# Two-bit threshold search, one packing pass and experts spread over the attention steps

## The reference

```python
xn = _layernorm(x)                                  # x: 1 x 2048 x 128
q, k, v = split(xn @ W_attn.T + b_attn)             # 16 heads of 8
att = softmax(where(causal, q @ k.T / sqrt(8), -inf))
y = (att @ v) @ W_proj.T + b_proj
probs = softmax(xn @ choice_w.T)                    # 2048 x 8
G, I = top_k(probs.T, 512)                          # per expert
h = silu(xn[I] @ w1)                                # 512 x 256, per expert
ffn = zeros.at[I].add(G[..., None] * (h @ w2))
out = x + y + ffn
```

## Time and profile before

| | us |
|---|---|
| median of 3 runs (361.47 to 363.31) | 362.79 |
| the profiled execution | 363.24 |
| its span | 361.5 |
| granted clock of TensorE, mean | 0.947 |

### The profile page before, as it was taken

One profiled execution on the slowest core, in us unless ns is written; L12 is line 12 of the kernel. 1 busy time (PEld: TensorE's weight loads), 2 busy tenths in 40 slices (PEclk: granted clock), 3 DMA queues, 4 the chain that ended last, 5 costly groups with the idle time before them and its releaser, 6 DMA issues.

```text
span 361.5 us, 6404 instructions
## 1 busy us (share of the span) xinstructions
PE 309.8 (86%) x2453; PEld 106.4 (29%) x2453; DVE 214.9 (59%) x558; ACT 289.5 (80%) x328; POOL 127.4 (35%) x122
## 2 busy tenths in 40 slices
PE   1684839699899769897998999999999999999970
PEld 0442802122222212221223232423242333232470
DVE  6939995966765878759777443251345433426443
ACT  1197747589999859897999999899999999998700
POOL 8520241920000000008760007584868251606060
PEclk9999558789999989999999999999999999999995
DMA  6035376720110210004342103352445231312057
GB/s 175 0 132 161 100 265 265 223 86 0 54 40 28 90 38 25 30 3 134 102 116 84 46 25 51 67 98 68 69 111 117 61 78 15 53 41 24 7 93 232
DMA packets 33683, 30.76 MB, mean 85 GB/s; under 512 B 3688, under 2 KB 28480, under 8 KB 33648
## 3 DMA queue, kind: packets, MB, share of 16 engines
q1 hardware_dynamic: 27248, 24.00, 20.7%
q0 software_dynamic: 6400, 6.30, 11.0%
HBM read 14.36 MB, written 15.93 MB: 84 GB/s over the span
## 4 chain that ended last, share of the span: by engine, by line
PE 60%; DVE 20%; ACT 9%; issue 5%; DMA 3%; POOL 1%; POOLq 1%; DVEq 0%; SPq 0%; ACTq 0%
PE bank L1178 29%; PE bank L1160 15%; ACT probs L703 6%; DVE probs L1010 5%; PE bank L1248 5%; PE bank L1240 4%; DVE onehot L951 2%; PE bank L1212 2%; PE bank L1122 2%; DVE y_acc L1027 2%; DMA xn<-total_dram 1%; DVE xn L736 1%; DVE cand L905 1%; PE bank L1187 1%; PE bank L1086 1%
## 5 line engine op out<-in xcount | busy, mean ns | idle before, releaser
L703 ACT ACTIVATE probs<-bank 128x1024 f32<-128x1024 f32 x272 | 255.9, 1070 | 31.6 <-PE bank L1160 31.2
L1178 PE MATMUL bank<-probs,v_grp 128*32 128x512 f32 (+3 forms) x1280 | 149.7, 551 | 14.2 <-DVE probs L1010 13.6
L1160 PE MATMUL bank<-q_aug,k_aug 51*128 51x512 bf16 (+3 forms) x640 | 89.3, 359 | 0.9 <-ACT probs L703 0.6
L608 POOL DMA_INDIRECT total_dram<-m_space,token x32 | 50.8, 1589 | 83.8 <-DVE m_space L996 76.5
L1010 DVE TENSOR_TENSOR probs<-probs,causal 128x512 f32<-128x512 f32 (+1 forms) x80 | 45.3, 586 | 30.3 <-ACT probs L703 30.3
L1160 PEld LDWEIGHTS bank<-q_aug,k_aug 51*128 51x128 bf16 x640 | 22.3, 95 | 114.7 <-ACT probs L703 93.0
L1178 PEld LDWEIGHTS bank<-probs,v_grp 128*32 128x32 f32 x1280 | 30.0, 110 | 58.1 <-issue 17.3
L951 DVE TENSOR_SCALAR onehot<-slot_iota,slot 128x512 bf16<-128x512 f16 x128 | 37.9, 363 | 6.9 <-PE bank L1212 6.6
L585 POOL DMA_DIRECT2D w_x<-in_L_ffn_w_dram x8 | 7.6, 944 | 87.8 <-DVE gate L970 87.7
L588 POOL DMA_INDIRECT parts<-xn_dram,token x32 | 32.1, 1003 | 9.7 <-issue 9.7
L984 DVE COPY m_space<-bank 128x512 f32<-128x512 f32 x16 | 11.0, 687 | 23.9 <-PE bank L1240 23.9
(11 more groups left out here) (128 smaller groups left out, 237.6 us busy)
## 6 DMA issues: line engine op xcount, KB each, us to landing
y_dram<-y_acc SPq DMA_DIRECT2D x16, 256.0 KB, 2.3
q_aug<-product_dram SPq DMA_DIRECT2D x32, 96.0 KB
k_aug<-product_dram SPq DMA_DIRECT2D x32, 96.0 KB, 2.2
w_x<-in_L_ffn_w_dram POOLq DMA_DIRECT2D x16, 128.0 KB
product_dram<-parts SPq DMA_DIRECT2D x4, 384.0 KB, 3.0
product_dram<-parts SPq DMA_DIRECT2D x6, 256.0 KB, 2.9
product_dram<-parts SPq DMA_DIRECT2D x2, 768.0 KB, 4.7
x_sb<-in_L_attn_x_dram SPq DMA_DIRECT2D x4, 256.0 KB, 3.5
```

Of the source, the lines that this page charges most:

```text
L608: pool.indirect_dma_start(total_dram, bass.IndirectOffsetOnAxis(ap=token[:, e, t:t + 1], axis=0), y_exp[:, e % 2, t, :], None, compute_op= ...
L703: act.activation(dst, src, ACT.Exp, scale=SCALE).then_inc(s_exp, 1)
L1160: last = pe.matmul(scores[(NU * g + u) % SB][:, a, at:at + width], k_aug[HEAD_ROWS[a], p, j * P:(j + 1) * P], q_aug[HEAD_ROWS[a], p, c * N ...
L1178: last = pe.matmul(acc[32 * h:32 * h + 32, first:first + width], v_grp[:, j, h, :], probs[:, (NS * g + k) % PB, h, at:at + width], start=( ...
```

## The change

1. **Search by two bits.** 15 rounds instead of 30, one per step, in steps 0 to 15 of group 0, half steps among them. Each round compares with three candidates at once (NV = 3): three DVE shifts, one comparison of 384 elements, one count of 384 columns, one sum, one compare-multiply, and a maximum over four.
2. **One packing pass.** Marks at step 16, ranks at 17, packing at steps 18 to 34, lists at 35, all in group 0. The slot is split into its tile of 128 (`high`) and its place in it (`low`). The payload, 5 wide instead of 32 and not filled with zeros any more, is multiplied by a mask of the own tile (`placed`). A one-hot of 128 places is the weights of a matmul with 20 columns, for 8 experts per step.
3. **Experts spread.** Expert e starts at step 40 + 12 e, counted over all groups, its pieces two steps apart; the last piece is at step 134 of 0 to 143.
4. **Order on VectorE.** In all groups the mask of the next step comes ahead of the piece of search, routing or expert.

The diff, cut to its core. Constants and POOL:

```diff
-    EPP = 4
-    PASSES = E // EPP
+    XB = 4
+    RADIX = 2
+    NV = (1 << RADIX) - 1
+    ROUNDS = BITS // RADIX
+    SEL_AT = ROUNDS + 1
+    RANK_AT = SEL_AT + 1
+    PACK_AT = RANK_AT + 1
+    LIST_AT = PACK_AT + NT + 1
+    EXPERT_AT, EXPERT_APART = LIST_AT + 5, 12
+    for _e in range(E):
+        _x, _h0, _h1, _y0, _y1 = [clear_of_half(EXPERT_AT + EXPERT_APART * _e + d) for d in (0, 2, 4, 8, 10)]
...
-    PK_P, PK_N, PK_GATE, PK_W = 0, 1, 2, 32
+    PK_P, PK_N, PK_GATE, PK_W = 0, 1, 2, 5
...
-            pool.memset(payload[:, :, :, :], 0.0).then_inc(s_route, 1)
```

VectorE's search and, behind the five rank operations, its routing:

```diff
             def search(k):
...
+                if k in range(1, ROUNDS + 1):
+                    old, new = cand[:, (k - 1) % 2], cand[:, k % 2]
                     dve.wait_ge(s_count, k)
+                    counts = spare[:, 0:NV * NT * E].rearrange("p (v n e) -> p v e n", v=NV, e=E)
+                    search_step(dve.reduce_sum(passed[:, :, :], counts, AX.X))
+                    search_step(dve.scalar_tensor_tensor(out=old[:, 1:, :], in0=passed[:, :, :],
+                                                         scalar=TOPK - 0.5, in1=old[:, 1:, :],
+                                                         op0=ALU.is_ge, op1=ALU.mult))
+                    dst = new[:, 0, :] if k < ROUNDS else thr[:, :]
+                    search_step(dve.reduce_max(dst, old.rearrange("p v e -> p e v"), AX.X))
+                if k in range(ROUNDS):
+                    own = cand[:, k % 2]
+                    for v in range(1, NV + 1):
+                        last = dve.tensor_scalar(own[:, v, :].bitcast(I32), own[:, 0, :].bitcast(I32),
+                                                 v << (BITS - RADIX * (k + 1)), None, ALU.bitwise_or)
+                    search_step(last)
+                    dve.tensor_tensor(above[:, :, :, :],
+                                      r_p[:, :, :].unsqueeze(1).broadcast_to([P, NV, NT, E]),
+                                      own[:, 1:, :].unsqueeze(2).broadcast_to([P, NV, NT, E]), ALU.is_ge)\
+                       .then_inc(s_above, 1)
...
             def route(k):
...
+                    slot_step(dve.tensor_copy(slot_int[:, :, :], slot[:, :, :]))
+                    dve.tensor_scalar(part_int[:, 0, :, :], slot_int[:, :, :], P - 1, None, ALU.bitwise_and)
+                    slot_step(dve.tensor_scalar(part_int[:, 1, :, :], slot_int[:, :, :], 7, None,
+                                                ALU.logical_shift_right))
+                    dve.tensor_copy(low[:, :, :], part_int[:, 0, :, :])
+                    slot_step(dve.tensor_copy(high[:, :, :], part_int[:, 1, :, :]))
+                    for t in range(SLOT_TILES):
+                        last = dve.tensor_scalar(own_tile[:, :, :, t], high[:, :, :], float(t), None, ALU.is_equal)
+                    slot_step(last)
+                n = k - PACK_AT
+                if n in range(NT):
+                    if n >= 2:
+                        dve.wait_ge(s_pack, n - 1)
+                    if n % PIECE_N == 0:
+                        ns = slice(n, n + PIECE_N)
+                        shape = [P, PIECE_N * E, SLOT_TILES, PK_W]
+                        dve.tensor_tensor(
+                            placed[:, ns].rearrange("p n e t w -> p (n e) t w"),
+                            payload[:, ns].rearrange("p n e w -> p (n e) w").unsqueeze(2).broadcast_to(shape),
+                            own_tile[:, ns].rearrange("p n e t -> p (n e) t").unsqueeze(3).broadcast_to(shape),
+                            ALU.mult)
+                    dve.tensor_tensor(onehot[:, n % 2, :, :], lane[:, :].unsqueeze(1).broadcast_to([P, E, P]),
+                                      low[:, n, :].unsqueeze(2).broadcast_to([P, E, P]), ALU.is_equal)\
+                       .then_inc(s_onehot, 1)
```

VectorE's order in a group, and TensorE's packing:

```diff
-                    if k in turns and turn_first:
-                        turn(turns.index(k))
                     if k + 1 < NS:
                         mask(g, k + 1)
-                    if k in turns and not turn_first:
-                        turn(turns.index(k))
+                    search(NS * g + k)
+                    route(NS * g + k)
+                    expert(NS * g + k)
...
             def route(k):
...
+                n = k - PACK_AT - 1
+                if n in range(NT):
+                    pe.wait_ge(s_onehot, n + 1)
+                    w = SLOT_TILES * PK_W
+                    for e in range(E):
+                        last = pe.matmul(spare[:, w * e:w * (e + 1)], onehot[:, n % 2, e, :],
+                                         placed[:, n, e, :, :].rearrange("p t w -> p (t w)"),
+                                         start=(n == 0 and e == 0), stop=(n == NT - 1 and e == E - 1),
+                                         skip_group_check=True)
+                    last.then_inc(s_pack, 1)
```

More of the change, by code:

```diff
@@ L289, in block_kernel @@
         s_basesent = sem("residual_in_dram")
-        s_got = [sem(f"expert_loaded{i}") for i in range(EPG)]
+        s_got = [sem(f"expert_loaded{i}") for i in range(XB)]
         s_xgT_ps = sem("gathered_transposed")
@@ L595, in _ @@
             pool.wait_ge(s_basesent, 16)
-            for e in range(EPG):
-                if e % EPP == 0:
-                    pool.wait_ge(s_token, e // EPP + 1)
+            pool.wait_ge(s_token, 1)
+            for e in range(XB):
                 fetch(e)
@@ L957, in route @@
-                if k == PACK_TURN[-1] + NT + 1:
-                    read_lists(PASSES - 1)
-            def read_lists(s):
-                dve.wait_ge(s_list, s + 1)
-                lists = spare.rearrange("p (t a w) -> p a t w", t=SLOT_TILES, a=EPP)
-                es = slice(EPP * s, EPP * (s + 1))
-                slot_step(dve.tensor_copy(slot_p[:, :, :], lists[:, :, :, PK_P]))
-                dve.scalar_tensor_tensor(out=token[:, es, :], in0=lists[:, :, :, PK_N], scalar=float(P),
-                                         in1=slot_p[:, :, :], op0=ALU.mult, op1=ALU.add)
-                slot_step(dve.tensor_copy(gate[:, es, :], lists[:, :, :, PK_GATE + 2]))
-                for i in (1, 0):
-                    last = dve.tensor_tensor(gate[:, es, :], gate[:, es, :], lists[:, :, :, PK_GATE + i], ALU.add)
-                    if i == 1:
-                        slot_step(last)
-                last.then_inc(s_token, 1)
@@ new lines, in route @@
+                if k == LIST_AT:
+                    dve.wait_ge(s_pack, NT)
+                    slot_step(dve.tensor_copy(packed[:, :, :, :], spare[:, 0:E * SLOT_TILES * PK_W].rearrange(
+                        "p (e t w) -> p e t w", e=E, t=SLOT_TILES)))
+                    dve.scalar_tensor_tensor(out=token[:, :, :], in0=packed[:, :, :, PK_N], scalar=float(P),
+                                             in1=packed[:, :, :, PK_P], op0=ALU.mult, op1=ALU.add)
+                    slot_step(dve.tensor_tensor(gate[:, :, :], packed[:, :, :, PK_GATE + 2],
+                                                packed[:, :, :, PK_GATE + 1], ALU.add))
+                    dve.tensor_tensor(gate[:, :, :], gate[:, :, :], packed[:, :, :, PK_GATE], ALU.add)\
+                       .then_inc(s_token, 1)
@@ L1037, in group @@
                             invert(i)
-            group(THRESHOLD_G, SEARCH_STEPS, search, turn_first=True)
-            group(ROUTE_G, ROUTE_STEPS, route, turn_first=True)
-            for g in range(EXPERT_G, G):
-                group(g, EXPERT_STEPS, lambda i: expert(g - EXPERT_G, i))
+            for g in range(G):
+                group(g)
             def normalise(c):
@@ L1199, in route @@
                       .then_inc(s_rank, 1)
-                for s in range(PASSES):
-                    n = k - PACK_TURN[s] - 1
-                    if n in range(NT):
-                        i = NT * s + n
-                        if i == 0:
-                            pe.wait_ge(s_payload, 1)
-                        if n == 0 and s > 0:
-                            pe.wait_ge(s_token, s)
-                        pe.wait_ge(s_onehot, i + 1)
-                        for a in range(EPP):
-                            last = pe.matmul(spare[PK_W * a:PK_W * (a + 1), :], payload[:, n, EPP * s + a, :],
-                                             onehot[:, i % 2, a, :], start=(n == 0), stop=(n == NT - 1))
-                        last.then_inc(s_pack, 1)
-                    if n == NT:
-                        pe.wait_ge(s_packread, s + 1)
-                        for t in range(SLOT_TILES):
-                            last = pe.transpose(spare[:, t * P:(t + 1) * P], packed[:, t * P:(t + 1) * P],
-                                                ident[:, :])
-                        last.then_inc(s_list, 1)
@@ L1233, in expert @@
                     last.then_inc(s_xgT_ps, 1)
-                if stage in H_TURN:
-                    f = H_TURN.index(stage)
+                for f, e in turns_of("h", at):
                     if f == 0:
@@ L1259, in scores_ahead, with group @@
```

(13 more changed lines are left out.)

185 lines of the change are left out of this document (80 added, 105 removed).

## The result

The changed kernel takes 369.02 us (median of 4 runs, 368.09 to 369.83) where the kernel before took 362.5 beside it (361.47 to 363.31): **1.018 times as long, interval 1.0144 to 1.0217**. The forecast was 374 with a range of 362 to 384: the direction and most of the places were right, the size was 5 us too high.

A forecast was written before the change was run, and what follows sets the result against it. ACT's exponentials were taken to bound the kernel, with PE also nearly full. Terms +11 + 9 + 5 - 12 + 2 - 4 = +11 took the span from 361.5 to 372.5 us; forecast 374 us, range 362 to 384.

The forecast's parts named there:

- search: Group 0, 15 two-bit rounds: each a closed PE-DVE loop of 2.36 us, longer than ACT's 1.83 us step; +11 us (7 to 16).
- entry: Group 0, steps 16 to 21: marking, ranking and first one-hot among masks make PE wait before packing; +9 us (6 to 13).
- packing: Group 0 from step 21: eight load and matmul pairs make PE's step 2.19 us against ACT's 1.83; +5 us (1 to 10).
- groups 1 to 3: Packing gone and experts spread: -12 us (-7 to -15), +1 for token lists, +1 for expert 0's fetch (0 to 3).
- end: After the last group: last y piece 16 us earlier, output adds end at about 354.5 instead of 358.6; -4 us (-3 to -5).
- 5.6 us later: Group 0, behind the first pack: steps 20 and 21 follow after 5.6 us (pack, copy 0.69, one-hot 1.2).
- I take 0.08, near the lower end: Time per pair of weight load and 20-column matmul, between 0.07 and 0.14 us; 0.65 us for a step's eight pairs.
- One-hot: DVE, 1024 elements at the rate of one, 1.2 us; at the rate of two 0.7, the change some 2 us cheaper.
- two signs: Right: group 0 some 97 to 100 us, groups 1 to 3 69 to 71 each; wrong: group 0 below 85, or those above 73.
- (1): Rival, faster, 356 us: a round takes 2.0 us; search costs 6, entry 6, packing 1, spreading brings 15, end 5; chance 0.12.
- (3): Rival, slower still, 384 us: the clock falls in plain search steps too, some ten steps at 1.1 us more each; chance 0.12.
- (2): Rival, near nothing, 363 us: round and packing less 4, spreading brings 15, entry 6 because ACT's three scored units cover it; chance 0.14.

The follow-up runs named there:

- one_bit: The changed kernel with 30 one-bit search rounds, ranking and packing at the change from group 0 to 1, experts closer together from step 55: 372.20 us, ratio 1.025.
- best: The changed kernel with one-bit rounds outside half steps and ahead of the mask, ranks at step 39, packing from 41, experts spread behind it: 358.60 us, ratio 0.987.
- experts_late: The changed kernel with the experts back at their places of the kernel before, in groups 2 and 3: 373.20 us, ratio 1.025 to the kernel before.

## Why the prediction was right, and where not

| term | forecast | measured |
|---|---|---|
| search | +11 | +10.5 |
| entry | +9 | +6.4 |
| packing | +5 | +0.5 |
| groups 1 to 3 | -10 | -8.9 |
| end | -4 | -3.6 |
| sum | +11 | +4.9 |

**Search: right, step by step.** Round 2.36 forecast, 2.39 measured. Count 3 comes 2.6 us later (2.8); steps 4 to 6 take 8.1 us (8.1), steps 7 to 10 with their masks 12.5 (12.6), steps 11 to 15 13.4 (11.8 and the 2 us allowed for a fall of the clock, which came from 81.4 to 88.2 and made the rounds up to counts 11 and 12 longer than 2.39 by 0.9 and 0.6). By one_bit, 8.7 of the 10.5 are the wider round.

**Entry: the mechanism right, the term too large by 2.6** (2.4 before the 8.8 was rounded to 9)**.** The wait stands where it was put, and its parts fit: threshold 1.4, marks 1.8 (1.9), rank block 3.3 (3.6), masked payload and one-hot 2.0; the first pack 11.5 us behind the count (11.8). From the first pack to the values of step 21 I had 6.4, and 2 more for the half clock; it took 6.36 in all. The clock did fall, to half from 105.3 to 112.1. What it cost can be read against `best`, which does the same steps (pack, values, scores, pack, values, copy) at full clock: its pack starts at 138.49 and the copy at 141.23, 2.7 us later:

```profile
138.49 0.36 PE L1231 MATMUL bank<-parts,onehot 128*128 128x20 bf16 x8 [0.45 <-DVE onehot L993]
```

Here it is 107.20 and 111.39, 4.2 us:

```profile
107.52 1.93 PE L1200 MATMUL bank<-probs,v_grp 128*32 128x384 f32 x16
...
111.39 0.69 DVE L1052 COPY y_acc<-bank 128x512 f32<-128x512 f32 x1 [2.51 <-PE bank L1200]
```

So the fall cost 1.5, near the 2 allowed; the step that failed is the "5.6 us later" for steps 20 and 21, which by this comparison would have been about 1.5 us less at full clock. The second one-hot (107.67 to 108.89) ran beside the values, so that the next pack did not wait.

**Packing: mis-sized, and the largest error.** The step that failed is "I take 0.08, near the lower end": a pair of a 128-column bf16 load and a 20-column matmul took 0.037 us, half of the lower bound of 0.07 that I drew from 256-column f32 pairs. Eight f32 loads and matmuls take 0.64 us with 256 moving columns and 1.06 with 512, so their time goes with the columns, and with 20 of them the bound from below was none. PE's step became 1.83 us instead of 2.19, so eleven steps stayed at ACT's pace. Of the 6.1 us by which the sum was too high packing is 4.5, the entry 2.6 and the search 0.5; groups and end, too hopeful by 1.5, take back a part.

**One-hot: right.** It took 1.219 us for 1024 results. The masked payload, also with a repeated operand, took 0.82 us for 640 (1.28 ns each), and sel_sum, two packed 16-bit tensors, 0.30 us for 272. The Trainium skill, VectorE: DVE Perf Modes, section What auto-detection actually checks, wants step 1 of every tensor for two results a cycle; the trace agrees, by the rate of one for the two with a repeated value.

**Groups: right sum, wrong reason in part.** I took the 12 us as packing gone and experts made cheaper by more room. experts_late shows nothing of the second inside the groups, and packing to be worth 9.4. That the sum came out near is in part luck. The start of group 1 took back some of it: lists, tables and five masks in one row on VectorE, PE idle 2.23 us, and the clock at 0.50 from 142.8 to 149.6; I had 1 us for it. So group 1 took 73.9 us, beyond the 69 to 71 that I named as a sign of being right and beyond the 73 that I named as a sign of being wrong; group 0, at 92.7, fell between its two signs (97 to 100, and 85).

**End: right** (-3.6), and it is all that spreading brings.

**Rivals.** (1) needed a round near 1.83 us; it was 2.39. (3) needed the clock to fall in plain search steps. It stayed at 1.00 while PE was busy 12.8 of 17.1 us with a pause in every round:

```profile
88.19:105.26 17.07, 12.83 (x100) 2.73 (x96) 13.15 (x49) 15.09 (x16) 0.00 (x0) 1.00 0.05 13
```

(2), near nothing, was nearer than the forecast in two of its terms: search and packing together 12 (measured 11.0) and the entry 6 (6.4). It failed by the spreading, 15 where groups 1 to 3 gave 8.9, and its reason for the entry did not hold: ACT ran out of scores and waited 5.17 us at 110.03.

## What to carry to other kernels

Work that closes a loop over two engines costs nothing while the loop fits into the step of the engine that bounds, and its whole excess per round once it doesn't: 15 two-bit rounds, each some 0.5 us too long, lost 8.7 us against one-bit rounds in the same steps, the same rounds in every second step lost at most 0.8. Before one wait is moved, list what stands in the waited-for engine's queue at the new place; a third buffer and one more step of lead took away what moving the block by two steps had only renamed. Test "spread" and "gone" apart: here all the gain inside the groups came from the work that went away.

## What the runs showed of the hardware

- Eight pairs of a weight load of 128 bf16 columns and a matmul of 20 columns delay what follows by 0.29 us, 0.037 us a pair, though the page of the profile gives one such matmul a mean of 0.174 (L1228): durations of pairs can't be added up, their pitch has to be read from the next instruction's start.
- Dependent small VectorE instructions start 0.22 to 0.24 us apart at 0.18 to 0.20 us each (L921, L925, L929), while the three independent ones of L929 take 0.32 together.
- The same length of half clock, 6.8 us, cost 1.4 us in the search (rounds of 3.27 and 2.95 us instead of two of 2.39) and 1.5 at the entry, though at half clock a values block takes 1.94 us instead of 1.07. The likely reason, which no run isolates, is that a part of the slower work filled waits that were there anyway.
- An 8-element VectorE shift took 2.05 us beside a POOL fill of 3.51 us, and 0.17 away from it (100.93, L905); both ended within 0.03 us of each other.
